# A feature-interaction tower on one core: which PSUM banks the turned features and the factors leave through

## The reference, cut to what matters

```python
e = stack([tbl_f[ids[:, f]] for f in range(39)], axis=1)       # (512, 39, 16), f32
x0 = xi = e
for W in (W0, W1):                                             # (39*39, 128), (39*128, 128)
    z = einsum('bmd,bnd->bdmn', x0, xi).reshape(b, d, -1)
    xi = einsum('bdp,po->bod', z, W)                           # a map (batch, 128, 16)
    res.append(xi)
z = sum(concatenate(res, axis=1), axis=-1)                     # (512, 256)
h = relu(concatenate([z, dense_ctx], 1) @ W_top1 + b_top1)     # 512 wide
y = relu(h @ W_top2 + b_top2) @ W_top3                         # 256 wide, then 1
```

## Time and profile before

| what | us |
|---|---|
| median of 3 runs (230.84 to 231.04) | 230.86 |
| the profiled execution's own time | 228.88 |
| its span, first to last instruction | 227.1 |
| PE busy, matmuls | 204.3 (90%) |
| DVE busy | 176.5 (78%) |
| ACT busy | 167.4 (74%) |
| POOL busy | 107.7 (47%) |

### The profile page before, as it was taken

One profiled execution on the slowest core, in us unless ns is written; L12 is line 12 of the kernel. 1 busy time (PEld: TensorE's weight loads), 2 busy tenths in 40 slices (PEclk: granted clock), 3 DMA queues, 4 the chain that ended last, 5 costly groups with the idle time before them and its releaser, 6 DMA issues.

```text
span 227.1 us, 4760 instructions
## 1 busy us (share of the span) xinstructions
PE 204.3 (90%) x1715; PEld 156.5 (69%) x1715; DVE 176.5 (78%) x295; ACT 167.4 (74%) x300; POOL 107.7 (47%) x106
## 2 busy tenths in 40 slices
PE   4598756879989998999999899999999999999995
PEld 4598623436555566777777578677778888889794
DVE  0789976999869899999988999898899787532010
ACT  5897765769777999689879998797877575775003
POOL 3787777777777777777877787000000000000000
DMA  5960000240292691200240000004000000000000
GB/s 139 204 145 10 9 6 7 65 69 7 60 253 64 118 284 17 40 10 6 66 64 9 6 9 6 1 3 104 13 3 0 0 3 0 1 0 3 0 0 0
DMA packets 22014, 10.24 MB, mean 45 GB/s; under 512 B 11576, under 2 KB 20877, under 8 KB 21992
## 3 DMA queue, kind: packets, MB, share of 16 engines
q1 hardware_dynamic: 18728, 9.11, 16.6%
q0 software_dynamic: 3264, 0.84, 4.0%
HBM read 8.63 MB, written 1.31 MB: 44 GB/s over the span
## 4 chain that ended last, share of the span: by engine, by line
PE 59%; POOL 15%; issue 10%; ACT 7%; DVE 5%; DMA 3%; SPq 1%; DVEq 0%; ACTq 0%
POOL feat L387 15%; PE s_bank L1013 14%; PE side_bank L967 6%; PE side_bank L969 6%; PE side_bank L968 6%; PE g_bank L995 4%; PE side_bank L995 3%; PE b_bank L947 3%; PE side_bank L934 2%; PE side_bank L962 2%; PE side_bank L975 2%; DMA g<-small 2%; DVE z_lo L796 2%; PE side_bank L912 2%; DVE z L786 1%
## 5 line engine op out<-in xcount | busy, mean ns | idle before, releaser
L387 POOL DMA_INDIRECT feat<-tbl,ids_sb x102 | 107.5, 1054 | 33.3 <-issue 23.8
L575 ACT ACTIVATE z_hi<-z 128x512 fp32r<-128x512 f32 x100 | 61.9, 633 | 10.6 <-DVE z L786 8.6
L786 DVE TENSOR_TENSOR z<-factors,b_bank 128x512 f32<-128x512 f32 x84 | 57.2, 682 | 7.9 <-PE b_bank L947 3.7
L796 DVE TENSOR_TENSOR z_lo<-z,z_hi 128x512 fp32r<-128x512 f32 x84 | 57.8, 689 | 0.3 <-ACT z_hi L575 0.2
L1013 PE MATMUL s_bank<-g,w_sb 128*128 128x128 f32 x312 | 47.5, 279 | 0.0
L1013 PEld LDWEIGHTS s_bank<-g,w_sb 128*128 128x128 f32 x312 | 44.1, 192 | 4.8 <-issue 2.4
L967 PE MATMUL side_bank<-z_hi,w_hi 128*128 128x512 f32 x84 | 42.3, 504 | 0.0
L969 PE MATMUL side_bank<-z_hi,w_lo 128*128 128x512 f32 x84 | 33.2, 396 | 0.0
L968 PE MATMUL side_bank<-z_lo,w_hi 128*128 128x512 f32 x84 | 32.9, 392 | 0.0
L467 ACT ACTIVATE factors<-side_bank 128x512 f32<-128x512 f32 x31 | 18.4, 594 | 7.2 <-PE side_bank L934 7.2
L947 PE MATMUL b_bank<-xs,sel 117*128 117x512 bf16 x48 | 18.7, 389 | 1.4 <-DVE direct_z L786 0.8
(11 more groups left out here) (181 smaller groups left out, 333.7 us busy)
## 6 DMA issues: line engine op xcount, KB each, us to landing
w_sb<-w SPq DMA_DIRECT2D x3, 832.0 KB, 6.8
feat<-tbl,ids_sb POOLq DMA_INDIRECT x102, 2.4
lines<-line SPq DMA_DIRECT2D x4, 320.0 KB, 2.2
diag<-lines SPq DMA_DIRECT2D x32, 40.0 KB, 2.2
wt_sb<-wt SPq DMA_DIRECT2D x2, 512.0 KB
g<-small SPq DMA_DIRECT2D x1, 770.0 KB
g<-small SPq DMA_DIRECT2D x1, 448.0 KB
w0p<-w_pair SPq DMA_DIRECT2D x1, 448.0 KB
```

What stands on the lines that cost most here:

```text
L387: nc.gpsimd.indirect_dma_start(feat[:, bt % 2, n * D:(n + 1) * D], None, tables[order[n]], bass.IndirectOffsetOnAxis(ids_sb[:, bt, n:n + 1 ...
L575: nc.scalar.activation(z_hi[:, s % RING, :], z[:, at, :], ACT.Copy).then_inc(rounded, 1)
L786: nc.vector.tensor_tensor(target, one, other, ALU.mult).then_inc(product, 1)
L796: nc.vector.tensor_sub(low[rows, s % RING, :], z[rows, SPLITS[s] % Z_RING, :], z_hi[rows, s % RING, :].bitcast(f32)).then_inc(remainder, 1)
```

## The change

There are now three lists of jobs that leave through banks which the pooled sums use as well. Turned half 0 goes through `g_banks[0]`, half 1 through `turn_bank`; factor `a` goes through `g_banks[1]`, factor `b` through `turn_bank`. The lists of the two banks of the pair wait only for the first of the two copies of the pooled sum (`freed` takes one from the count); `turn_bank` waits for both as before. `g_block` waits for the fills of all three lists. And within a chunk `a` is filled at offset 3 and `b` at offset 4, where it was `b` and then `a`, on PE and ACT alike.

```diff
-FILL_A = 4
-FILL_B = 3
+FILL_A = 3
+FILL_B = 4
...
-        turn_banks = [turn_bank, g_banks[1], l1_bank[1], b_bank[1][:]]
+        turn_banks = [turn_bank, g_banks[1], g_banks[0], l1_bank[1], b_bank[1][:]]
+        freed = [0, 1, 1]
...
-        fills = [[("x", 0, 0)], [("x", 0, 1)], [("a", 0, 0)], [("b", 0, 0)]]
-        fills_before_g, g_before_fill = [], [0]
+        fills = [[("x", 0, 0)], [("x", 0, 1)], [], [("a", 0, 0)], [("b", 0, 0)]]
+        x_home, home = [2, 0], {"a": 1, "b": 0}
+        fills_before_g, g_before_fill = [[] for _ in freed], [[0] * len(jobs) for jobs in fills[:len(freed)]]
+
+        def fill_next(k, job):
+
+            fills[k].append(job)
+            g_before_fill[k].append(len(fills_before_g[k]))
+
         for s in range(LAST):
             bt, v = divmod(s, SPT)
             if bt + 1 < TILES:
                 for k, at in enumerate(X_AT[bt + 1]):
                     if v == at:
-                        fills[0].append(("x", bt + 1, k))
+                        fill_next(x_home[k], ("x", bt + 1, k))
...
             if chunk_at(s, G_AT) is not None:
-                fills_before_g.append(len(fills[0]))
...
+                for k, counts in enumerate(fills_before_g):
+                    counts.append(len(fills[k]))
+            for name, at, next_at in (("a", FILL_A, A_AT), ("b", FILL_B, B_AT)):
+                if (i := chunk_at(s, at)) is not None and (i + 1) % CPT:
+                    fill_next(home[name], (name, i + 1, 0))
+                if bt + 1 < TILES and v == next_at[bt + 1]:
+                    fill_next(home[name], (name, CPT * (bt + 1), 0))
...
                 if n:
                     pe.wait_ge(turn_taken[k], n)
-                if k == 0 and g_before_fill[n]:
-                    pe.wait_ge(g_copied, GPC * g_before_fill[n])
+                if k < len(freed) and g_before_fill[k][n]:
+                    pe.wait_ge(g_copied, GPC * g_before_fill[k][n] - freed[k])
...
-                pe.wait_ge(turn_taken[0], fills_before_g[i])
+                for k, counts in enumerate(fills_before_g):
+                    if counts[i]:
+                        pe.wait_ge(turn_taken[k], counts[i])
...
+                if (i := chunk_at(s, FILL_A)) is not None and (i + 1) % CPT:
+                    fill_factor("a", i + 1)
                 if (i := chunk_at(s, FILL_B)) is not None and (i + 1) % CPT:
                     fill_factor("b", i + 1)
-                if (i := chunk_at(s, FILL_A)) is not None and (i + 1) % CPT:
-                    fill_factor("a", i + 1)
```

More of the change, by code:

```diff
@@ L295, in build @@
         kept = sem("kept")
-        turn_filled = [sem(f"turn_filled{k}") for k in range(4)]
-        turn_taken = [sem(f"turn_taken{k}") for k in range(4)]
+        turn_filled = [sem(f"turn_filled{k}") for k in range(5)]
+        turn_taken = [sem(f"turn_taken{k}") for k in range(5)]
         chunk0_taken = sem("chunk0_taken")
@@ L340, in build @@
                     if v == at:
-                        fills[0].append(("x", bt + 1, k))
-            g_before_fill += [len(fills_before_g)] * (len(fills[0]) - len(g_before_fill))
+                        fill_next(x_home[k], ("x", bt + 1, k))
             if chunk_at(s, G_AT) is not None:
-                fills_before_g.append(len(fills[0]))
-            if (i := chunk_at(s, FILL_B)) is not None and (i + 1) % CPT:
-                fills[0].append(("b", i + 1, 0))
-            if (i := chunk_at(s, FILL_A)) is not None and (i + 1) % CPT:
-                fills[0].append(("a", i + 1, 0))
-            if bt + 1 < TILES and v == A_AT[bt + 1]:
-                fills[0].append(("a", CPT * (bt + 1), 0))
-            if bt + 1 < TILES and v == B_AT[bt + 1]:
-                fills[0].append(("b", CPT * (bt + 1), 0))
-            g_before_fill += [len(fills_before_g)] * (len(fills[0]) - len(g_before_fill))
+                for k, counts in enumerate(fills_before_g):
[5 more added lines that the diff above has]
+                    fill_next(home[name], (name, CPT * (bt + 1), 0))
         fill = {job: (k, n) for k, jobs in enumerate(fills) for n, job in enumerate(jobs)}
@@ L658, in _ @@
                     take_xit(i)
+                if (i := chunk_at(s, FILL_A)) is not None and (i + 1) % CPT:
+                    take_factor("a", i + 1)
                 if (i := chunk_at(s, FILL_B)) is not None and (i + 1) % CPT:
                     take_factor("b", i + 1)
-                if (i := chunk_at(s, FILL_A)) is not None and (i + 1) % CPT:
-                    take_factor("a", i + 1)
                 if 1 <= bt < TILES - 1:
@@ L762, in _ @@
             dve.wait_ge(*after(turn_filled, "b", 0, 0))
-            nc.vector.tensor_copy(factors[:, 0, 1, :], b_bank[1][:]).then_inc(turn_taken[3], 1)
+            nc.vector.tensor_copy(factors[:, 0, 1, :], b_bank[1][:]).then_inc(turn_taken[fill["b", 0, 0][0]], 1)
             def multiply(s):
@@ L987, in g_block @@
                     pe.wait_ge(embedded, embeds[2])
-                    pe.wait_ge(*after(turn_taken, "x", 0, 1))
                 side = [l1_bank[i % 2], turn_bank] if i % 2 == 0 else [turn_bank, l1_bank[i % 2]]
```

## The result

| | before | changed |
|---|---|---|
| median, us (6 runs each) | 230.95 (229.46 to 233.71) | 233.76 (231.84 to 234.19) |
| profiled execution: time, span | 228.88, 227.1 | 233.82, 232.2 |
| ratio of the runs | | 1.0131, 95% interval 1.0098 to 1.0164 |
| 102 gathers, busy us | 107.5 | 113.6 |
| the last gather ends | 141.27 | 147.31 |

The change is 1.3% slower. Before's six runs are the three named above and three later ones. The prediction was 230.0 in a range of 229.4 to 231.1, so it missed in sign and in size.

The account below looks back on a forecast made before the run. POOL's chain of gathers was taken to pin the program at 142.7 us, so only later savings counted: 0.59 + 0.29 - 0.01 = 0.87 us, from 230.86 to 230.0 us, in a range of 229.4 to 231.1.

Parts of the forecast that it names:

- Part 1: Factor fills no longer wait for the other factor's copy; up to 1.44 us saved before 142 us, booked as 0.
- the pin: POOL's chain of gathers in tile 3, whose last gather lets DVE start at 142.7 us; savings before it count 0.
- Parts 2, 3 and 4: Tile 3: half 0 waits for one pooled-sum copy, 0.59; half 1 not for half 0's take, 0.29; `a` after both, -0.01.
- part 4: Tile 3: factor `a` still needs both halves taken; it fits by 0.09 us, and 0.01 is taken off.
- Part 5: Tile 2's savings and DVE's earlier `a` lie before the pin; behind 151 us PE is full: 0.
- Part 6: Two more waits before each of 15 pooled sums and at first-chunk factors: 0, upper bound 0.48 us over six sums.
- Part 7: POOL's queue has no instruction moved and its waits are met long before; one gather changing length shifts the chain 1.05 us.
- the prediction's own sign: In tile 3: the prediction is wrong if the last gather's landing moved by more than 0.3 us.
- The rule that I weighed and dropped: SBUF port lock: a denser DVE would lengthen the gathers; set aside for the row of 138.03, where a gather took 0.95 us.
- Rival B: POOL's chain in tile 3: gathers run longer, 1.05 us each; by two, 232.1 us, slower by 0.5%; chance 0.08.
- Rivals A, C and D: A: gain given back in tile 3, 230.9, chance 0.16; C: added waits cost, 230.5, 0.05; D: gathers shorter, 228.95, 0.06.

## Why the prediction was wrong

- **Part 1 (factor fills, 0 before the pin).** The waits are gone, and without the gathers some 0.9 us of them are gained, within the bound of 1.44. That DVE's wait for the last gather came to 2.31 us, where about 2 was predicted, is luck: the data landed 6.04 us later, and the swap alone, which keeps the PE waits (5.0 us in 6), has 2.29.
- **Parts 2, 3 and 4 (0.59 + 0.29 - 0.01).** Right to 0.08 us: 0.95 behind the pin, each start within 0.08 us of where it was put, counted from the pin. The margin of part 4 held.
- **Part 5 (the swap and tile 2: 0).** Behind the pin the swap is worth nothing, as said. Wrong in what it left out: what lies before the pin moves DVE against the gathers. With the swap alone the chain is 2.1 us longer than in before's profile, and the median 1.0 us higher.
- **Part 6 (added waits: 0).** Right: of the six pooled sums behind 151 us, five start 0.33 us behind the matmul before them and the last 0.45, in both kernels.
- **Part 7 (POOL unchanged) is the step that failed.** "Its queue has no instruction moved" was true and beside the point, for the length of a gather is set by what DVE runs when it starts. I had the pin right, and took its position as given: booked at 0, it moved by 6.04 us in the profiles, with 28 long gathers for 14. By the prediction's own sign (a landing moved by more than 0.3 us) it was wrong.
- **The rule that I weighed and dropped.** The subtraction of the earlier trace rows starts 0.53 us behind the gather of 138.03, beyond the moment that counts, and the gather of the earlier trace rows next to it starts 0.12 us behind the product of 139.16. One row that agreed with me was read; the 101 others stood in the same trace. The Trainium skill (SBUF — State Buffer, "SBUF: two separate sides") says that VectorE with two SBUF inputs and a GpSimd instruction that reads SBUF exclude each other, and 471 of 472 long gathers bear that out for the gather. Of descriptor writing the same section says that it starves under a two-port instruction, and that a plain `tensor_tensor` was not seen to stall a DMA; the prediction ran the two together, and the subtractions here, plain ones, do hold gathers up. It takes no denser DVE either, as I had it: DVE was less busy than before in two of the three stretches up to 142 us. Its "for the whole instruction" the rows don't bear out: DVE's subtraction of 138.56 ran in 0.69 us while a gather was under way.
- **Rival B** had the right place, and long gathers as the means, but put them down to shifted traffic; it had a chance of 0.08 and a price of two gathers (2.1 us). In the profiles it was 6.0 us in all, against typical runs about 3.9 (147.3 less the 143.4 us at which the kernel before would end its chain at its median of 230.95, by 85.8 behind it and 1.75 between span and time). 3.9 - 1.0 = 2.9, and the medians differ by 2.8. "The three runs agree within 0.2 us, so the chain does not wander" fell as well: the later runs of the same kernel reach from 227.88 to 234.14 us.
- **Rivals A, C and D** got no support: nothing was given back behind the pin, the added waits cost nothing, and the chain as a whole became no shorter. Single gathers did: the last took 0.94 us in place of 2.00.

What stays open is why the changed kernel lands on the long chain in most of its runs. The rule tells which gathers are long once DVE's schedule is known, though not at the edge and not always by how much; but DVE's schedule waits for the gathers in turn, and I found no short way to say beforehand where the two settle.

## What to carry to other kernels

Where POOL's transfers pin the end, cost them against DVE's schedule: for each, ask whether DVE is in an instruction with two SBUF inputs when it starts, and take a range as wide as moving that schedule by a few tenths makes it. A gain in front of such a chain, or any edit that moves DVE, may redraw its length, here by 2 to 6 us in the profiles and 1 to 3 in the medians, against a gain of 1. Before reordering for less than that, loosen the pin: a later use of the gathered data (0.9 us here), or fewer two-input instructions (2.4 us less in one kernel, 1.4 more in the other), and judge by many runs and not by one profile.

## What the hardware showed unasked

A gather of 128 rows takes 0.94 us undisturbed, needs 0.82 us once DVE lets it go, and can be held up by two instructions in a row (2.08 us above). A 128x512 f32 subtraction or product on DVE that starts up to 0.05 us before a gather takes 0.73 us in the median in place of 0.68. The gaps between gathers stayed 0.30 us whatever was named as their releaser. The part of the program behind the last gather is constant to 0.2 us in kernels of one kind (85.7 to 85.9 us in six that keep before's banks, 84.8 to 84.9 us in nine profiles with the whole change, but for those split two steps later). So most of a program's spread of 4 us from run to run probably sits in the chain in front of it, though only one run of each has a profile.
